# Early-fusion block with sixteen top-k experts: all engines ordered by global steps, two look-up banks, attention in the transposes' bank

## The reference

```python
h = concat([patches @ proj_w.T + proj_b, txt], axis=1)            # (16, 113, 192)
h = h + attention(layernorm(h))       # 12 heads of 16, a scale per head; diagonal masked but for token 0
x = layernorm(h)
pe = softmax(posembed @ pos_w + pos_b)                            # (16, 192)
y = (silu(x @ sg_w) * (x @ su_w)) @ sd_w                          # shared, 384 wide
for i in range(16):                                               # experts
    gate = (x * pe[i]) @ gate_w + gate_b                          # (1808, 192)
    top, where = top_k(gate, 96)
    z = take_along_axis(x, where) * softmax(top)                  # (1808, 96)
    y += (silu(z @ eg_w[i]) * (z @ eu_w[i])) @ ed_w[i]
out = h + (silu(layernorm(y) @ m1_w + m1_b) @ m2_w + m2_b)
```

## Time and profile before

| | |
|---|---|
| median of three runs | 2830.11 us |
| profiled execution's own time | 2832.04 us |
| its span | 2830.2 us |
| VectorE busy | 2502.2 us, 88% |
| TensorE matmul busy, weight load busy | 2311.0 us (82%), 1277.1 us (45%) |
| ScalarE, GpSimd busy | 1752.6 us (62%), 1725.8 us (61%) |
| mean granted TensorE clock | 0.815 of 2.4 GHz |

### The profile page before, as it was taken

How to read it: one execution, slowest core, us unless ns; L and a number is a source line. 1 busy time by engine, 2 the same in 40 slices (tenths; PEclk the granted TensorE clock), 3 DMA queues, 4 the chain that set the end, 5 groups by cost and what they waited for, 6 DMA issues and landing times.

```text
span 2830.2 us, 49810 instructions
## 1 busy us (share of the span) xinstructions
PE 2311.0 (82%) x12378; PEld 1277.1 (45%) x12378; DVE 2502.2 (88%) x13377; ACT 1752.6 (62%) x3995; POOL 1725.8 (61%) x2202
## 2 busy tenths in 40 slices
PE   4389888888877887889788888898889777888796
PEld 3245444444444454445444444454445334444344
DVE  3779599899999998999998979999989999999970
ACT  2144666666766656667666566675666665666664
POOL 1134666566666666667566566675666766676675
PEclk9567988788989778979798778896887987887877
DMA  1213222222212212222222121212122221212210
GB/s 58 57 17 79 50 49 54 45 48 51 49 46 52 48 46 53 48 52 49 47 52 49 44 55 43 57 46 50 39 43 55 58 59 34 57 45 51 59 41 20
DMA packets 192965, 138.25 MB, mean 49 GB/s; under 512 B 107763, under 2 KB 180430, under 8 KB 192678
## 3 DMA queue, kind: packets, MB, share of 16 engines
q1 hardware_dynamic: 191204, 132.28, 20.9%
q0 software_dynamic: 928, 1.72, 0.2%
q10 hardware_dynamic: 546, 1.06, 0.1%
HBM read 105.04 MB, written 27.77 MB: 47 GB/s over the span
## 4 chain that ended last, share of the span: by engine, by line
DVE 41%; PE 34%; ACT 8%; DMA 6%; issue 5%; POOL 5%; SPq 2%; ACTq 0%; POOLq 0%
DVE idx L573 14%; DVE keys L575 14%; DVE vals L569 12%; PE ps L1119 8%; PE ps L1196 3%; PE ps L1130 3%; PE ps L1085 3%; PE ps L1176 3%; PE ps L1105 3%; DMA nt_gate<-normt_d 2%; PE ps L1044 2%; ACT looked_s L705 2%; ACT code L694 2%; PE ps L1168 2%; PE ps L1025 2%
## 5 line engine op out<-in xcount | busy, mean ns | idle before, releaser
L942 POOL TENSOR_TENSOR picked<-looked_s,code 128x384 f32<-128x384 f32 (+1 forms) x912 | 815.9, 906 | 373.3 <-ACT looked_s L705 372.2
L573 DVE FIND_INDEX8 idx<-vals,keys 128x8 uint16<-128x192 f32 x2712 | 942.0, 348 | 0.0
L1119 PE MATMUL ps<-code,table 128*128 128x384 bf16 (+1 forms) x2736 | 707.9, 375 | 282.9 <-ACT looked_s L705 214.8
L569 DVE MAX8 vals<-keys 128x8 f32<-128x192 f32 x2712 | 821.9, 343 | 41.6 <-ACT keys L661 41.6
L575 DVE MATCH_REPLACE8 keys<-vals,keys 128x192 f32<-128x192 f32 x2486 | 842.3, 339 | 0.0
L694 ACT ACTIVATE code<-ps 128x768 bf16<-128x768 f32 (+1 forms) x912 | 736.2, 807 | 153.9 <-PE ps L1105 131.9
L705 ACT ACTIVATE looked_s<-ps 128x384 f32<-128x384 f32 (+1 forms) x912 | 445.1, 488 | 357.1 <-PE ps L1119 342.4
L1119 PEld LDWEIGHTS ps<-code,table 128*128 128x128 bf16 x2736 | 255.0, 107 | 596.8 <-issue 430.9
L1105 PE MATMUL ps<-rows,codew 17*128 17x384 bf16 (+1 forms) x1824 | 342.9, 373 | 89.4 <-ACT code L694 59.2
L904 POOL TENSOR_TENSOR prod_s<-gu_s 96x256 f32<-96x256 f32 x256 | 184.8, 722 | 339.8 <-ACT gu_s L740 329.8
L1105 PEld LDWEIGHTS ps<-rows,codew 17*128 17x128 bf16 x1824 | 87.8, 93 | 442.0 <-ACT code L694 224.4
(11 more groups left out here) (149 smaller groups left out, 2497.2 us busy)
## 6 DMA issues: line engine op xcount, KB each, us to landing
wexp<-in_w_exp SPq DMA_DIRECT2D x60, 576.0 KB, 5.1
wdown<-in_w_down SPq DMA_DIRECT2D x60, 576.0 KB, 6.6
digit_d<-dcode SPq DMA_DIRECT2D x56, 384.0 KB, 2.6
rows<-digit_d SPq DMA_DIRECT2D x224, 96.0 KB
table<-parts SPq DMA_DIRECT2D x240, 9.0 KB
hr<-norm_d SPq DMA_DIRECT2D x112, 12.0 KB
patch<-in_patches SPq DMA_DIRECT2D x16, 108.0 KB, 5.1
tok_d<-h SPq DMA_DIRECT2D x16, 84.8 KB
```

The lines of the kernel that those rows point to most:

```text
L569: nc.vector.max(vals[:, par, e, at], from_keys[:, e, :]).then_inc(chain, 1)
L573: found = nc.vector.max_index(idx[:, par, e, at], vals[:, par, e, at], from_keys[:, e, :])
L942: nc.gpsimd.tensor_tensor(picked[:, o % PICKS, w], looked_s[:, o % 4, w], code[:, o % 4, 1, w], ALU.mult).then_inc(picked_ready, 1)
L1119: ins = nc.tensor.matmul(ps[:, LOOK_B, w], table[:, o, s, :], code[:, o % 4, 0, w], start=(s == 0), stop=(s == 2))
```

## The change

Steps are counted through all blocks (step = 16n + o), and each engine has one function `step_work(step)` that looks its work up in tables.

- `look` alternates between two banks (1 and 2) and waits for the copy two looks back. Attention gives up bank 2 and shares MISC_B with the transposes and the final layers, under one counter `misc_out`. Gates leave MISC_B and share GU_B with the MLP units, under one counter `gu_out`.
- ScalarE and GpSimd do `activate`, `keys_out`, `turned_out` and `hide` one step after the matmuls (attention's copies were there before). `DOWN_LAG` is 4 (was 3).
- The first two codes of the next block are made at steps 14 and 15; the last `put`, the open `down`s, scaling (step 1), weighting (step 1) and `invert` (step 2) move into the next block. The turn is at step 3 (was 2).
- An image starts every 52 steps, not 48, and its stages take the next free odd or even step of a list per g (four places at g = 1, seven elsewhere). Image 2's turn_h is at step 45 (was 38).
- `score_max` comes after a round computed from the step of s2.
- The tile's gates for g = 3 are made at steps 1 and 3 of its own g = 0 block; the others at 3, 7, 11 of the g = 2 and g = 3 blocks. The wait for `nt_gate` is at the first gate (step 3), and SP issues `load_gate` ahead of the expert weights; `wexp` is reloaded after its last `up`, `wdown` after its last `down`.
- The rest's band 1 comes ahead of band 0, and weights 8 to 15 are loaded first, which saves one reload of all.

```diff
-SPAN = 3
-PE_AT = dict(zip(STAGES, [0, 3, 5, 7, 9, 11, 13, 15, 24, 26, 28, 30, 33, 35, 38]))
+GAP = {"turn_x": 4, "t0": 9, "turn_o": 4, "turn_h": 4}
+PERIOD = 52
+FREE = {None: [0, 2, 4, 6, 8, 10, 12, 14], 0: [1, 5, 7, 9, 11, 13, 15], 1: [1, 5, 7, 13],
+        2: [1, 5, 7, 9, 11, 13, 15], 3: [1, 5, 7, 9, 11, 13, 15]}
...
+def max_after():
+    spots = {}
+    for i in range(2, IMAGES):
+        rounds = 2 * ROUNDS * (ATT_PE[i, "s2"] + 5 - 8) // OCT + 2 * (2 * ROUNDS)
+        block, r = divmod(rounds, 2 * ROUNDS)
+        spots[block, r // ROUNDS, r % ROUNDS] = i
+    return spots
...
-GATE_SPOTS = {3: (0, 0), 6: (0, 1), 11: (1, 0), 14: (1, 1)}
+UNIT_SPOTS = {0: [5, 8, 11, 14], 1: [1, 3, 5, 8, 11, 14], 2: [5, 9, 13, 15], 3: [5, 9, 13, 15]}
+TAIL_SPOTS = [5, 7, 9, 11]
+GATE_SPOTS = {0: {1: (3, 0), 3: (3, 1)}, 1: {}, 2: {3: (0, 0), 7: (0, 1), 11: (1, 0)}, 3: {3: (1, 1), 7: (2, 0), 11: (2, 1)}}
+FINAL_PE = {9: 0, 11: 1, 15: 2}
...
                 def look(n, o):
-                    if n or o:
-                        pe.wait_ge(looked_out, OCT * n + o)
+                    if n or o >= 2:
+                        pe.wait_ge(looked_out, OCT * n + o - 1)
...
                 def gate(t, g, pair):
-                    pe.wait_ge(keys_ready, pairs_before(t, g) + pair)
+                    bank = MISC_B if (t, g, pair) in EARLY_GATES else GU_B
+                    pe.wait_ge(gu_out, keys_of(t, g, pair) - 1)
+                    if (g, pair) == (0, 0):
+                        pe.wait_ge(nt_gate_in, 16 * t)
...
+                def step_work(step):
+                    n, o = divmod(step, OCT)
+                    if 0 < n <= LAST + 1 and o == 0:
+                        put(n - 1, OCT // QUADS - 1)
+                    if n <= LAST and o % QUADS == 2 and o > 2:
+                        put(n, (o - 2) // QUADS - 1)
+                    if step in TURN_AT:
+                        turn_x(TURN_AT[step])
+                    if step in GATE_AT:
+                        gate(*GATE_AT[step])
+                    if step in UNIT_AT:
+                        up(*UNIT_AT[step])
+                    if step - DOWN_LAG in UNIT_AT:
+                        down(*UNIT_AT[step - DOWN_LAG])
...
+                    if step in PE_STAGE:
+                        attend(*PE_STAGE[step])
```

More of the change, by code:

```diff
@@ L82, in stages_at @@
[L82 to L96, removed]
+    return FIRST_BANKS[k % len(FIRST_BANKS)] if k < len(FIRST) else MISC_B
 def octet(o):
     return OCT // QUADS * (o % QUADS) + o // QUADS
-REST_LIST = [(0, "band", 0), (1, None, 0), (2, None, 1), (3, "band", 1)]
@@ new lines, with block_no, unit_steps @@
+REST_GATES = {3: (2, 0), 7: (2, 1)}
+TURN = 3
+DOWN_LAG = 4
+PREPARE = 8
+FINAL_PE = {9: 0, 11: 1, 15: 2}
+FINAL_ACT = {3: "y", 4: "square", 6: "norm", 10: "zt", 12: "st1", 16: "out"}
+FINAL_POOL = {3: 0, 4: 1, 12: 2, 17: 3}
+def block_no(t, g):
+    return 0 if t == 0 else BPT * (t - 1) + g + 1
+def unit_steps():
+    at = {}
+    for n in range(1, LAST + 2):
+        t, g = tile_of(n)
+        tm, units = (t if g else t - 1), units_of((g - 1) % BPT)
+        if tm == 0:
+            units = REST_LIST
+        for (u, e, half), spot in zip(units, TAIL_SPOTS if n > LAST else UNIT_SPOTS[g]):
+            at[OCT * n + spot] = (tm, u, e, half)
+    return at
@@ new lines @@
+TURN_AT = {OCT * (n + 1) + TURN: n for n in range(LAST + 1)}
+FINAL_PE_AT, FINAL_ACT_AT, FINAL_POOL_AT = final_steps(FINAL_PE), final_steps(FINAL_ACT), final_steps(FINAL_POOL)
+EARLY_GATES = [(0, 0, 0), (1, 0, 0), (1, 0, 1), (1, 1, 0), (1, 1, 1)]
+GU_USES = [("gate",) + use for use in EARLY_GATES]
+GU_USES += [use for step, use in sorted([(s, ("gate",) + x) for s, x in GATE_AT.items()] +
+                                        [(s, ("unit", x[0], x[1])) for s, x in UNIT_AT.items()])]
+GU_NTH = {use: k + 1 for k, use in enumerate(GU_USES)}
@@ new lines @@
+MISC_USES = [("stage",) + pair for pair in FIRST]
+MISC_USES += [use for step, use in sorted([(s, ("stage",) + x) for s, x in PE_STAGE.items()] +
+                                          [(s, ("turn", n)) for s, n in TURN_AT.items()] +
+                                          [(s, ("final",) + x) for s, x in FINAL_PE_AT.items()])]
+MISC_NTH = {use: k + 1 for k, use in enumerate(MISC_USES)}
+assert len(GU_NTH) == len(GU_USES) and len(MISC_NTH) == len(MISC_USES)
+assert not set(UNIT_AT) & set(GATE_AT)
@@ L124, in slots @@
+assert not set(TURN_AT) & set(PE_STAGE) and not set(FINAL_PE_AT) & set(PE_STAGE) and not set(FINAL_PE_AT) & set(TURN_AT)
 def slots(slot):
@@ L831, in _ @@
                 slots(slot)
-                turned_out(LAST)
-                for u, e, half in units_of(BPT - 1):
-                    activate(TILES, u, e)
-                y_taken(TILES)
-                for step in range(5):
-                    final(TILES, step)
+                for step in range(AFTER, AFTER + 2 * OCT + 2):
+                    step_work(step)
             @block.gpsimd
@@ L943, in slot @@
                                                 ALU.mult).then_inc(picked_ready, 1)
[L944 to L961 removed]
+                        step_work(OCT * n + o)
                 def final(t, step):
@@ L1002, in _ @@
                 slots(slot)
-                for u, e, half in units_of(BPT - 1):
-                    hide(TILES, u, e)
-                for step in range(4):
-                    final(TILES, step)
+                for step in range(AFTER, AFTER + 2 * OCT + 2):
+                    step_work(step)
             @block.tensor
@@ L1257, in slot @@
-                    put(n, OCT // QUADS - 1)
-                    for (u, e, half), spot in zip(units, spots):
-                        if spot + DOWN_LAG >= OCT:
-                            down(tm, u, e, half)
+                        elif n < LAST:
+                            make_code(n + 1, o + 2 - OCT)
+                        step_work(OCT * n + o)
                 pe.wait_ge(pe_in, PE_IN)
```

420 lines of the change are left out of this document (202 added, 218 removed).

## The result

The changed kernel takes 2680.05 us in the median (2668.87 to 2705.19, four runs) against 2829.55: ratio 0.947, 95% interval 0.943 to 0.951. The forecast was 2698, the likeliest case's range 2660 to 2725. The profiled execution took 2678.3 us, its span 2676.5.

The account below looks back on a forecast made before the run. VectorE was taken to bound the kernel, but for recurring waits. Terms: 315 up to block 5, 2282 of VectorE's work, 15 of waits, 86 of tail, together 2698 us; likeliest case 2660 to 2725, whole range 2650 to 2765.

Parts of the forecast that it names:

- Which engine bounds: From block 5 on, VectorE sets the pace at about 44 us a block; TensorE's loop follows at 41 to 44.
- One sign: ScalarE's wait for digits, 69.9 us before in the attention stretch, would grow because the loop waits for VectorE.
- A: Stretch up to block 5's first VectorE operation: ends at 315 us, between 290 and 330, against 322.1 before.
- The sum's part on DMA: After image 2's last copy, ahead of block 5: 2 us issue, 8.5 store, 5 load, 4 gate and a copy step.
- I let two banks take 5 of the 11 idle us: Blocks 0 and 1: two look banks remove 5 of TensorE's 11 idle us, putting image 2's last copy at about 297.
- B: Block 5 to the close of block 56: 2282.0 us of VectorE's work, its score and key waits gone, plus 15 us.
- the 15 us for heavy blocks: Waits added between block 5 and block 56's close where heavy blocks miss the pace: 15 us, between 0 and 67.
- The loop's pace: TensorE's and ScalarE's loop with attention: from 45.7 us a block before to 41 to 44, against VectorE's 44.
- Between half and all of 131.1/36 = 3.6: Attention stretch: share of the looks' wait for the previous look's copy, in us a block, that the second bank removes.
- the weight-load rule of the Trainium skill: Weight-load occupancy, 47% in the attention stretch, shows ample TensorE room: no 15 us of waits, so 2683 us.
- The Trainium skill's remark on double-buffered PSUM: Cited against the second look bank: double-buffering gave another kernel no further gain; pace would be 44.4, sum 2698 us.
- C: Tail after VectorE closes block 56: 87.8 us before, 2 less with two look banks, so 86.

Follow-up runs that it names:

- the light kernels: Kernel before and changed kernel, each with VectorE reading 96 of the 192 keys so that it bounds nothing: 2727.27 and 2613.3 us.
- experiment 11: Changed kernel with image 2's stages, store and score exponentials brought forward and tile 2's first gate at step 13 of block 2: 2684.55 us, ratio 0.950.
- experiment 4: Changed kernel, VectorE whole, with all looks in one bank, each waiting for the copy of the one before: 2673.67 us, ratio 0.945.
- experiment 10: Changed kernel, VectorE whole, with score_max seven rounds (12.5 us) earlier: 2723.01 us, ratio 0.962.
- experiment 12: Changed kernel, VectorE whole, with one look bank and the unit, gate and turn copies and units' products back at their matmuls' step: 2689.24 us, ratio 0.950.
- experiment 1: Kernel before with score_max 9 us later in VectorE's order: 2750.24 us, ratio 0.970.
- experiment 9: Kernel before with score_max 9 us later, load_gate ahead of load_experts and the nt_gate wait at the first gate: 2710.55 us, ratio 0.955.
- experiment 5: Changed kernel with VectorE reading 96 of 192 keys and all looks in one bank: 2611.71 us, ratio 0.926.
- experiment 7: Changed kernel, VectorE reading 96 of 192 keys, with the last put, scaling and weighting back at the block's end: 2652.07 us, ratio 0.938.
- experiment 2: Kernel before with VectorE reading 96 of the 192 keys: 2727.27 us, ratio 0.959.
- experiment 3: Changed kernel with VectorE reading 96 of the 192 keys: 2613.3 us, ratio 0.924.

## Why the prediction was right, by its steps

*Which engine bounds: right.* VectorE has no wait from 324 us on, and the light kernels put the loop's pace at 42.7 against VectorE's 43.7. The whole kernel says the same: 43.7 less the wait for digits, 43.4/36 = 1.2, is 42.5. That the margin was small was right as well: in experiment 11, 17 us of an earlier start brought 12.3 us of waits. One sign failed. ScalarE's wait for digits was to grow and fell, from 69.9 us to 43.4. The sum itself should have said so: a loop at 42.5 behind a VectorE at 44 has some 1.5 us a block to wait, less than the 1.9 it had while VectorE stood still for scores.

*A, up to block 5: 324, forecast 315.* The sum's part on DMA held: the last copy of image 2 ended a chain in which the store no longer waits for SP's other work. It was shorter than forecast: the copy came at 305.6, the store went out 0.4 us later (2 forecast) and the load 5.7 after that (8.5), with the keys copied 11.9 us behind it (5 + 4 and a step). What was late is the copy, forecast at 297. "I let two banks take 5 of the 11 idle us" failed: TensorE's idle time in blocks 0 and 1 was 18.2 us (114.1 less 95.9), more than the 11.2 before. The new order moves work past the border of blocks 1 and 2, the band's `down` of 32 matmuls (5.4 us) among it; the two blocks took 114.1 us (117.3), and block 2 took 54.3 (47.2) with TensorE busy for 50.2 of them (35.4) at a granted clock of 0.78 (0.89). Much of this is this one execution. From 145 us to the start of block 5, in this trace and in that of experiment 4:

```profile
145.00:324.00 179.00, 156.00 (x829) 88.89 (x828) 141.08 (x765) 87.26 (x221) 81.38 (x115) 0.72 0.18 39
```

```profile
145.00:313.70 168.70, 144.47 (x831) 83.69 (x831) 141.52 (x769) 87.89 (x221) 81.47 (x115) 0.76 0.19 41
```

The same matmuls took 156.0 us at a clock of 0.72 and 144.5 at 0.76, and block 5 began at 324.0 and 313.7; in experiments 10 and 12 it began at 315.7 and 319.2, at 0.76 and 0.77. So 315 was a fair figure for this order.

*B: the waits taken as gone were gone, the 15 us for heavy blocks were nothing, and VectorE's own work was 14 us shorter.* The 132.1 of scores, the 6.2 of keys and the look's waits for `nt_gate` are all gone. The stretch took 2268.0 us, not 2282.0 + 15. VectorE's own work shrank by 14, from 2282 to 2268: the groups of VectorE there, first before, then after:

```profile
L545 DVE TENSOR_SCALAR ntop<-vals 128x4 f32<-128x4 f32 x52 | 23.9, 460 | 0.0
```

```profile
L606 DVE TENSOR_SCALAR ntop<-vals 128x4 f32<-128x4 f32 x53 | 14.1, 265 | 0.0
```

`ntop` alone gave back 9.8 us (median 159 and 158 ns, longest 2275 against 1105). I had counted it as fixed work. That the new order did it is not borne out. `ntop` over the whole span, in experiments 4 and 12, which have the new order too:

```profile
L606 DVE TENSOR_SCALAR ntop<-vals 128x4 f32<-128x4 f32 (+1 forms) x57 | 25.9, 455 | 0.1
```

```profile
L606 DVE TENSOR_SCALAR ntop<-vals 128x4 f32<-128x4 f32 (+1 forms) x57 | 27.1, 476 | 0.1
```

It was 24.7 us before and 14.7 in the changed kernel's trace. VectorE's stretch from block 5 to the close of block 56, less its waits, was 2275.2 us in experiment 4, 2272.1 in 10, 2276.5 in 11 and 2281.7 in 12, and 2268.0 is the shortest; with the old order it was 2282.0, and 2291.8 and 2283.1 in experiments 1 and 9. So some 8 of the 14 us belong to the one execution that was profiled, and the rest may be the new order's. Why `ntop` is at times ten times as long was not tried; the Trainium skill ("SBUF — State Buffer", SBUF: two separate sides) says that VectorE and GpSimd share a pair of ports as an exclusive lock, but no run here shows that this is it.

*The loop's pace: the number right, a term of it wrong.* "Between half and all of 131.1/36 = 3.6" for the second bank was nothing (experiments 4, 5). With it out, the terms named leave 45.7 - 1.3 + 1 = 45.4 us a block, and the loop took 42.7. So some 2.7 us a block came from parts that had no term. The open block borders are one: putting them back bare costs 39 us (experiment 7), but how much the borders of the kernel before cost is not shown. TensorE's own time is another: I took its 40.1 us a block as fixed, and it was 37.8, with 1% fewer matmuls and the granted clock at 0.89 for 0.83; whether the clock made the loop faster or rose with it was not tried. So the pace came out right partly by luck. The Trainium skill's remark on double-buffered PSUM ("TensorE: Matmul & The Clock Gate", HAM oscillation), cited against the change, was the better guide to that one term. With two banks the looks' wait went and the codes' wait of the same size came.

*By the weight-load rule of the Trainium skill* ("Perfetto Trace Analysis", Identifying the Most-Contended Engine) the 15 us were none, and they were none, in the whole kernel. In the light kernel, though, TensorE's matmul rows fill 1351.5 of 1537 us and the weight loads 761.7, and the loop is at its limit. So "ample room" is not shown.

*C: 84.5 us (2592.0 to 2676.5), forecast 86.*

The errors of the terms, measured less forecast: A +9, B -29, C -1.5, together -21.5, which is 2676.5 against 2698. A and B err in opposite directions, and both in part by what this one execution happened to do (a low clock ahead of block 5, a short `ntop` behind it), so part of how near the sum came is luck. The mechanism, that VectorE sets the pace once its waits are gone, is what experiments 1, 2, 3 and 10 show.

What stays open: how the light gain of some 100 to 114 us divides between the block borders, SP's order, the spreading of attention over 52 steps an image (which leaves less of it in each block), the new gate spots and the clock. They were not tried one by one.

## What to carry to other kernels

Where one engine should never stop, look first at each of its waits and at how late the waited-for thing is: here one instruction moved by 9 us gave half the gain (80 of 150 us), and a load put ahead of another in a queue, with its wait moved to the first use, 40 us more. Measure the supporting loop's own pace by making the bounding engine lighter; that tells whether a part helps, where the whole kernel hides it. Ahead of adding a second bank, look at what the copying engine does right behind the copy: here TensorE needed that just as soon, and the bank gave nothing. And compare several traces of one order before explaining 10 us: a clock or an instruction's length that differs between executions looks like an effect.

## What the runs showed of the hardware that was not expected

Nothing new of a mechanism. In size: an `ntop` of 4 elements a partition took 0.16 us in the median and up to 2.3 us, and its mean over the span was 258 ns in the changed kernel's trace, 434 in the kernel before's and 378 to 476 in four other traces with VectorE whole and the changed order (experiments 4, 10, 11, 12). Executions of the same changed kernel spread over 2669 to 2705 us, those of the kernel before over 2812 to 2854.
